# Row tiles of a mixture-of-experts loop loaded by transposing DMAs, with VectorE joining the 16-bit pieces and 15 tiles combined on TensorE

## What is computed

```python
logits = h @ gate_w.T                    # 2048 tokens, 32 experts
scores = sigmoid(logits)                 # groups of experts limit the choice
tki    = top 8 experts of each token     # tkw: their weights, scaled by 2.5
g = silu(einsum('th,eih->tei', h, w_gate))
u = einsum('th,eih->tei', h, w_up)
routed = einsum('tei,ehi->th', g * u * combine[:, :, None], w_down)
shared = (silu(h @ sh_gate.T) * (h @ sh_up.T)) @ sh_down.T
out    = x + routed + shared
```

## Time and profile before

| | |
|---|---|
| time, median of 3 runs | 613.6 us (612.79 to 614.25) |
| the profiled execution, its own time | 612.29 us |
| its span, first to last instruction | 611.0 us |
| mean granted TensorE clock | 0.976 |
| busy share PE / DVE / ACT / POOL | 92% / 67% / 61% / 59% |

### The profile page before, as it was taken

One profiled execution on the slowest core, in us unless ns is written; L12 is line 12 of the kernel. 1 busy time (PEld: TensorE's weight loads), 2 busy tenths in 40 slices (PEclk: granted clock), 3 DMA queues, 4 the chain that ended last, 5 costly groups with the idle time before them and its releaser, 6 DMA issues.

```text
span 611.0 us, 11524 instructions
## 1 busy us (share of the span) xinstructions
PE 563.9 (92%) x2677; PEld 422.3 (69%) x2677; DVE 407.4 (67%) x1554; ACT 372.3 (61%) x993; POOL 361.8 (59%) x414
## 2 busy tenths in 40 slices
PE   3989989889999798798997999999999999999996
PEld 2666557655766455555666888888788888888875
DVE  6975675986768987647776444444444444688897
ACT  1867888868786755552611666566566666677760
POOL 4343233632143377876777777777777777777730
PEclk9979999999999899899799999999999999999999
DMA  8999300000000023239364999876666666999966
GB/s 258 394 397 383 131 0 2 1 1 0 2 0 0 17 92 119 98 119 343 119 222 167 304 321 342 293 223 214 200 202 205 209 207 198 346 412 407 411 255 222
DMA packets 62063, 119.69 MB, mean 196 GB/s; under 512 B 8667, under 2 KB 45583, under 8 KB 59951
## 3 DMA queue, kind: packets, MB, share of 16 engines
q1 hardware_dynamic: 48079, 77.63, 37.5%
q0 software_dynamic: 13488, 41.04, 17.7%
q10 hardware_dynamic: 432, 0.29, 0.3%
HBM read 61.29 MB, written 57.64 MB: 195 GB/s over the span
## 4 chain that ended last, share of the span: by engine, by line
PE 78%; DVE 10%; ACT 6%; DMA 3%; issue 1%; POOL 1%; SPq 0%; DVEq 0%; POOLq 0%; ACTq 0%
PE ps L2023 22%; PE ps L2043 11%; PE ps L1671 7%; PE ps L1656 6%; PE ps L1882 5%; PE ps L1682 5%; PE ps L1695 5%; PE ps L2036 3%; PE ps L1642 3%; PE ps L1777 3%; PE ps L1783 2%; DVE tokrow L750 2%; PE ps L1794 2%; DMA arena<-yrows 2%; DMA xs<-in_x 1%
## 5 line engine op out<-in xcount | busy, mean ns | idle before, releaser
L2023 PE MATMUL ps<-arena,mats 128*128 x636 | 164.0, 381 | 0.3 <-issue 0.3
L609 POOL DMA_INDIRECT xrows<-tokrow,place_of x128 | 125.2, 978 | 41.8 <-issue 37.5
L1267 DVE TENSOR_TENSOR mats<-ps,mats 128x128 f32<-128x128 f32 x159 | 46.3, 291 | 106.1 <-ACT mats L1453 101.1
L2023 PEld LDWEIGHTS ps<-arena,mats 128*128 128x128 f32 x636 | 108.6, 191 | 8.8 <-issue 0.5
L2043 PE MATMUL ps<-arena,mats 128*128 x318 | 95.5, 383 | 1.0 <-DVE mats L1274 1.0
L1453 ACT ACTIVATE mats<-ps 128x128 f32<-128x128 f32 x159 | 44.1, 277 | 56.4 <-PE ps L2023 56.4
L1446 ACT COPY mats<-ps 128x256 f32<-128x256 f32 x159 | 58.0, 365 | 11.9 <-PE ps L1882 11.9
L1387 ACT ACTIVATE hat<-tokrow,total 128x256 f32<-128x256 f32 x96 | 47.6, 499 | 18.8 <-DVE tokrow L815 11.7
L1395 ACT ACTIVATE hat<-tokrow,shift,rstd 128x256 f32<-128x256 f32 x96 | 49.7, 591 | 12.9 <-POOL shift L540 12.8
L2043 PEld LDWEIGHTS ps<-arena,mats 128*128 128x128 f32 x318 | 48.0, 191 | 13.7 <-issue 2.1
L545 POOL TENSOR_SCALAR var_eps<-variance 128x4 f32<-128x4 f32 x24 | 6.4, 269 | 83.5 <-ACT hat L1387 83.2
(11 more groups left out here) (237 smaller groups left out, 1136.0 us busy)
## 6 DMA issues: line engine op xcount, KB each, us to landing
hat<-xrows SPq DMA_DIRECT2D x81, 160.0 KB
rows<-xrows SPq DMA_DIRECT2D x78, 160.0 KB
arena<-in_experts SPq DMA_DIRECT2D x4, 1920.0 KB, 18.8
xrows<-padrow SPq DMA_DIRECT2D x32, 160.0 KB
hat<-yrows SPq DMA_DIRECT2D x5, 1024.0 KB, 8.4
tokrow<-yrows SPq DMA_DIRECT2D x5, 1024.0 KB
hatT<-yrows SPq DMA_DIRECT2D x5, 1024.0 KB, 8.9
xrows<-padrow SPq DMA_DIRECT2D x1, 4960.0 KB
```

Of the source, the lines that this page charges most:

```text
L609: gp.indirect_dma_start(out=xrows[:, :], out_offset=bass.IndirectOffsetOnAxis(ap=place_of[:, g, k:k + 1], axis=0), in_=tokrow[:, g, :], in ...
L2023: mm = te.matmul(bank(6 + u)[:, 0:2 * I], turned_row[u][:, dc * P:(dc + 1) * P], arena[:, dc * D:(E - 1) * WCOL + (dc + 1) * D][:, bass.ds ...
```

## The change

1. **Row loads.** The 256 token values of a tile are loaded by `dma_start_transpose`, which works on 16-bit elements: a row is 512 halves, and the tile arrives as `[128 partitions, 4 chunks, 128 rows]` of halves, already turned. The 64 other columns come by a second, plain DMA. Each row load is thus two DMAs on the same queue, and a row buffer is ready at a count of 32 in place of 16.
2. **Halves.** For this, each token row is stored with all the low halves first and then all the high halves. ScalarE writes the normalised tokens into `hat` and a new operation `halve(i)`, once per block, rearranges 4 x 512 halves per partition into `tokrow`. `dispatch` and the first `shared_silu` of the block wait for it. TensorE turns the tokens from `hat`.
3. **TensorE** has no `turn_row` and no PSUM bank for it. `copy_row` is now the joining of the two halves of each value, SBUF to SBUF, 512 elements of 16 bits per partition with a step of two on the output; VectorE does it up to tile 134, ScalarE from tile 135 (`SHIFT_AT`). `copy_act` is ScalarE's for every tile.
4. **15 tiles kept.** `KEPT` goes from 6 to 15, so tiles 144 to 158 are not scattered. Their products (`combine`) stand inside TensorE's loop, two stages after `down`, with six sets of 0/1 matrices in turn.
5. **Tables.** `ASK_AT` and `SUM_AT` are set anew, ten token tiles are asked for after SyncE's last row load, and the last reload has no buffer of its own: it waits, as the others do, for the sum three tiles before it.

```diff
-KEPT = 6
-SHIFT_AT = 116
+KEPT = 15
+TOKEN_SETS = 6
+SHIFT_AT = 135
-ASK_AT = [128, 129, 133, 136, 139, 142, 145, 148, 152, 155, 158]
-SUM_AT = [120, 123, 126, 129, 132, 135, 138, 141, 145, 148, 151, 154]
+ASK_AT = [140, 141, 149, 156, 157, 158]
+SUM_AT = [133, 136, 142, 148, 149, 150, 152, 153, 155, 156, 157, 158]
...
                 if g == EARLY_SUMS:
                     wait_scattered(TILES - KEPT)
-                if g == EARLY_SUMS + 3:
-
-                    sy.wait_ge(down_done, TILES)
-                    sy.dma_start(last_back, results[g]).then_inc(row_in[0], 16)
-                    return
...
                 if n >= ROWBUFS:
-                    sy.wait_ge(row_turned, n - ROWBUFS + 1)
+                    sy.wait_ge(row_copied, n - ROWBUFS + 1)
                     sy.wait_ge(own_ready, (n - ROWBUFS) // GROUP + 1)
-                sy.dma_start(rowbuf[n % ROWBUFS], xrows[bass.ds(at[n % 4], P), :]).then_inc(row_in[n % ROWBUFS], 16)
+                sy.dma_start_transpose(rowhalf[n % ROWBUFS], halves[bass.ds(at[n % 4], P), 0:2 * D]
+                                       ).then_inc(row_in[n % ROWBUFS], 16)
+                sy.dma_start(rowbuf[n % ROWBUFS][:, WTS:ROW], xrows[bass.ds(at[n % 4], P), WTS:ROW]
+                             ).then_inc(row_in[n % ROWBUFS], 16)
...
+            def halve(i):
+                ac.wait_ge(normed[i // Q], past(i, 2 * ROUNDS, TQ))
+                ac.copy(slots[:, set_of(i), :].bitcast(HALF).rearrange("p t (h d) -> p t h d", h=2),
+                        hat[:, set_of(i), :].bitcast(HALF).rearrange("p t (d h) -> p t h d", h=2)).then_inc(halved, 1)
...
+            def copy_row(s):
+                u = s % 2
+                ve.wait_ge(row_in[s % ROWBUFS], 32 * (s // ROWBUFS + 1))
+                if s >= 2:
+                    ve.wait_ge(gate_up_done, s - 1)
+                ve.tensor_copy(turned_row[u].bitcast(HALF).rearrange("p (n h) -> p h n", h=2),
+                               rowhalf[s % ROWBUFS].rearrange("p (h c) r -> p h (c r)", h=2)).then_inc(row_copied, 1)
...
+            def combine(k):
+                n = TILES - KEPT + k
+                te.wait_ge(token_known, k + 1)
+                te.wait_ge(y_ready, n + 1)
+                for t in range(TQ):
+                    mm = te.matmul(bank(4 + t // 2)[:, t % 2 * D:(t % 2 + 1) * D], of_token[k % TOKEN_SETS][:, t, :],
+                                   ybuf[y_place(n)], start=k == 0 and t % 2 == 0, stop=k == KEPT - 1 and t % 2 == 1)
+                mm.then_inc(combined, 1)
...
-            for n in range(TILES + 3):
-                if 1 <= n < TILES:
-                    turn_row(n)
+            for n in range(TILES + 5):
...
+                if TILES - KEPT + 5 <= n:
+                    combine(n - 5 - (TILES - KEPT))
```

More of the change, by code:

```diff
@@ L7 @@
 I32 = mybir.dt.int32
+HALF = mybir.dt.uint16
 ALU = mybir.AluOpType
@@ L255, in build @@
             "p (k d) -> p k d", k=TOPK), hatT[0].rearrange("p c (k d) -> p (c k) d", d=D)]
-        last_back = place(arena, 0, TOPK, D)
         of_token = [part(hatT[1][:, :, :], k * TQ * P, TQ, P) for k in range(4)]
-        of_token += [part(tokrow[:, :, :], k * TQ * P, TQ, P) for k in range(KEPT - 4)]
+        of_token += [part(tokrow[:, :, :], k * TQ * P, TQ, P) for k in range(TOKEN_SETS - 4)]
         into_token = part(mats[:, 4, :, :], GROUP * E * 3, GROUP)
@@ L502, in sync_program @@
                 ask_back(g)
+                if g == T and T >= len(ASK_AT):
+                    store(0, TQ)
                 if g == EARLY_SUMS - 1:
@@ L605, in dispatch @@
                     gp.wait_ge(weighed, 2 * (i + 1))
-                    gp.wait_ge(normed[i // Q], past(i, 2 * ROUNDS, TQ))
+                    gp.wait_ge(halved, i + 1)
                 g = i * TQ + step // 4
@@ L1322, in add_kept @@
                 if half == 0:
-                    ve.wait_ge(combined, 1)
+                    ve.wait_ge(combined, KEPT)
+                    ve.wait_ge(out_ready, EARLY_SUMS + TQ)
                 g = EARLY_SUMS + 2 * half
-                at = (4 + 2 * half) * BANK
-                ve.tensor_tensor(xs[:, g:g + 2, :], ps[:, at:at + 2 * BANK].rearrange("p (b c) -> p b c", b=2)[:, :, 0:D],
-                                 xs[:, g:g + 2, :], ALU.add).then_inc(out_ready, 2)
+                ve.tensor_tensor(xs[:, g:g + 2, :], bank(4 + half).rearrange("p (t d) -> p t d", t=2),
+                                 xs[:, g:g + 2, :], ALU.add).then_inc(out_ready, 1)
             starts = [tiles_from(phase) for phase in range(3)]
             for n in range(TILES + 2):
+                if n < SHIFT_AT:
+                    copy_row(n)
                 if 1 <= n <= TILES:
@@ L1392, in normalise @@
                 ac.wait_ge(shift_ready[i // Q], past(i, n))
-                into = hat if n < 2 * ROUNDS else slots
                 for g in tiles_of(i):
-                    ac.activation(into[:, g, :], source[:, g, :], ACT.Identity, bias=shift[:, g:g + 1],
+                    ac.activation(hat[:, g, :], source[:, g, :], ACT.Identity, bias=shift[:, g:g + 1],
                                   scale=rstd[:, g:g + 1]).then_inc(normed[i // Q], 1)
@@ L1467, in copy_out @@
                     u = y_last(n) // YGROUP
-                    ac.wait_ge(scattered[u % YGROUPS], 16 * YGROUP * (u // YGROUPS + 1))
+                    ac.wait_ge(scattered[u % YGROUPS],
+                               16 * sum(m // YGROUP % YGROUPS == u % YGROUPS for m in range(min(YGROUP * (u + 1), TILES - KEPT))))
                 ac.wait_ge(own_ready, n // GROUP + 1)
@@ L1579, in scalar_program @@
             score_tokens(0)
+            halve(0)
             evacuate(3, 3)
@@ L1589, in scalar_program @@
             score_tokens(1)
+            halve(1)
             normalise(3, 4, slots)
@@ L1607, in scalar_program @@
             score_tokens(2)
+            halve(2)
             normalise(3, 2 * ROUNDS, xs)
@@ L1611, in scalar_program @@
             score_tokens(3)
+            halve(3)
             shared_silu(2, 1)
```

97 lines of the change are left out of this document (35 added, 62 removed).

## The result

| | before | changed |
|---|---|---|
| median (range, runs) | 613.92 us (612.79 to 616.09, 4) | 748.04 us (745.68 to 753.58, 4) |
| ratio | | 1.219 (95%: 1.211 to 1.227) |
| span, mean granted clock | 611.0 us, 0.976 | 748.1 us, 0.919 |

The forecast was 606.3 us with a range to 628. The change makes the kernel 22% slower; the prediction had given such a side a chance of 0.28 and no price over 653.

A forecast was written before the change was run, and what follows sets the result against it. TensorE and GpSimd were both taken as full and ending together; on GpSimd's path 611.0 - 11.4 + 1.1 + 3 = 603.7, plus 1.3 us twice, made 606.3 us, range 600.5 to 628.

The forecast's parts named there:

- I take it as hidden: SyncE's row loads: a pair hides up to 1.43 us a tile, so the transposing load was given no cost.
- The first rival: SyncE's queue or DMA engines: transposing loads set the pace from 1.48 us a pair, up to 652 us; chance 0.21.
- Up to about 1.0 fits beside the scatters: DMA engines: a tile's load takes 0.54 us of their time, and about 1.0 us would fit.
- TensorE would end at 586.1.: TensorE's kept products: end at 605.3, less 35.0 us of transposes, plus 15.8 us for nine more kept tiles.
- With the same 24.05 us behind it.: After the loop: last scatter starts at 575.6, the unchanged 24.05 us follow, and the span ends at 599.6.
- The GpSimd path: GpSimd's scatters to the end: nine fewer save 11.4 us, which limits the gain; 603.7 with the added costs.
- I take 3 us, near that row: GpSimd's DMAs beside VectorE's new row copy: total lengthening taken as 3 us, near the L804 row's no cost.
- as the adds: Row copy holding GpSimd's DMAs like VectorE's two-input adds: 0.05 to 0.15 us each, 7 to 23 us.
- The row of L804: VectorE's L804 beside a dispatch at 241.84, which keeps its 0.96 us: read as the copy costing GpSimd nothing.
- The second rival: VectorE's copy shuts GpSimd out for its whole length: +0.33 us for each of 150 DMAs, 653 us; chance 0.06.
- TensorE's tile of 1.40 and VectorE's chain: In the loop: TensorE's tile falls from 1.62 to 1.40 us; VectorE's chain of 1.3 to 1.9 mostly fits 1.77.
- the third rival: The loop doesn't reach 1.40: VectorE's chain leaves 1.44 to 1.47 us a tile, 614 us; chance 0.09.

The follow-up runs named there:

- plain_pair: The change with its transposing load replaced by a plain load of the same 256 columns, rows unturned: 640.08 us, ratio 1.045 to the kernel before.
- two_chunks: The change with the transposing load bringing two of four chunks and the copy reading a constant: 747.04 us, ratio 1.217 to the kernel before.
- values_on_scalar: The change in full, with the plain loads issued by ScalarE's queue and the transposing ones by SyncE's: 659.79 us, ratio 1.073 to the kernel before.
- early8_third: plain_early8 repeated beside a kernel before of 613.25 us: 632.90 us, ratio 1.031.
- copies_kept6_again: plain_pair with row copies on ScalarE, the sums' places of before and six kept tiles: 618.18 us against 615.36, ratio 1.0049.
- four_plain: plain_pair with the 256 columns brought by three plain loads, so four issues a tile: 767.6 us, ratio 1.251 to the kernel before.
- plain_early8: plain_pair with the sums and their loads placed earlier, nearly as before: 764.75 us beside a kernel before of 722.24 us, ratio 1.060.

## Why the prediction was wrong, point by point

- **"The transposing load may cost some 1.5 to 1.8 times a plain one before it counts. ... I take it as hidden."** This is the step that failed. The bound was right, 1.43 us a pair; the value inside it was a choice, without a row. The issue is 1.20 us, three times the 0.41 of the plain one next to it. In the prediction's own measure, from one start to the next, it is 1.41 us where 0.58 was a plain one's, and the pair with its register work is 2.0 to 2.4 where 1.43 would have been hidden. `plain_pair` shows that this is 108 us, `two_chunks` that half the bytes don't make the issue cheaper, `values_on_scalar` that 88 come back once the two loads have separate queues.
- **The first rival** had the mechanism, the place and the point of decision (1.48 us a pair), and its signature (a queue without gaps), but "at twice the plain issue" bounded the price at 1.74 a pair and 652 us. With the measured 2.18 of a tile without a pad its own formula gives 312 + 149 x 2.18 + 21.6 = 658 for tile 149 (its load is issued at 665.8), and with the 59 us that the forecast has behind it 717. So the price and the chance of 0.21 were wrong, and some 30 of the 748 us are again not in the formula: the chain that ended last has only reloads and VectorE's work from 684.80, where the row loads are nearly through, to the end, since ten token tiles are asked for after the last row load.
- **The bytes of the loads.** "Up to about 1.0 fits beside the scatters" was not the limit in the change (share 0.54). In `values_on_scalar` the share is 0.96, beside a queue that still hardly waits.
- **"TensorE would end at 586.1."** With free loads it ended at 628.7, 41.5 us late even after the 1.1 of `halve`. From the table: it starts 7.5 us later, not 1.1 (the first dispatch alone, which was taken as covered, starts at 213.4 in place of 210.58; where the rest comes from was not looked into); between tiles 0 and 130 it needs 194.6 us where 212.8 - 28.6 = 184.2 were counted, and between tiles 0 and 50 nearly nothing is gained (80.5 us against 81.8), while `pick` waits 8.9 us for plain loads among the pads; and behind tile 130 it needs 91.8 where 57.7 - 6.4 + 15.8 = 67.1 were counted. The nine kept tiles were sized about right, as `early8_third` has them (3.13 - 1.40 = 1.73 each against 1.755). What was missing is that TensorE can't use its lead: the two paths were summed as if independent, but y buffers and reloads tie it to GpSimd's scatters.
- **"With the same 24.05 us behind it."** True where six tiles are kept: 25.0 and 24.9. With fifteen it is 53 us in `plain_pair`, where the late reloads and sums come last, and 45 in `early8_third`, where TensorE's kept products do. The GpSimd path was counted with a tail that belonged to other places of the sums and another number of kept tiles.
- **"I take 3 us, near that row"** for VectorE's copy against GpSimd: measured 587.0 - 577.5 = 9.5 us at the last scatter, inside the 7 to 23 of "as the adds" and not near L804's nothing. The reckoning for the adds was the right one: hit by the share of time that a copy runs, 0.455/1.40, and held for half its length gives 0.07 us each, and the 89 DMAs from 410 to 530 are 0.08 longer on average. The row of L804 was misread. That operation starts at 242.06, 0.22 us after its dispatch, and so could not show a hold, while the add at 538.72 was running when its scatter started: it ends at 540.01, the scatter 0.82 behind it.
- **The second rival** charged each of 150 DMAs with a whole copy, 0.33 us; that price is refuted by the 0.08. The mechanism is not: a DMA that starts into a copy is held until the copy ends. The Trainium skill (SBUF — State Buffer, "SBUF: two separate sides") says that of a VectorE operation in a two-port mode and a GpSimd operation the one that starts first has the shared port pair for the whole instruction. The trace agrees, with the 49 held DMAs and the 67 of 76 that start before a copy and take less than 1.00; whether this copy runs in such a mode no run shows.
- **TensorE's tile of 1.40 and VectorE's chain**: right (501.55 and 502.95; 1.41 over long stretches of `plain_pair`), so the third rival is out. `copy_row` took 0.455 us in the bounds of 0.37 to 0.65.
- **Which path ends it.** That at most the GpSimd path's share of the 35 us would come through was right in kind, and too hopeful in size: `copies_kept6_again` is what remains, none.

## What to carry to other kernels

A DMA of a kind that the trace doesn't show has a price on the queue that issues it, apart from its bytes; if the loop's slack is known (here 1.43 us a tile), measure the issue first or let the range reach what three or four times a plain one would give. When two engines end together, freeing one gives little (here nothing), and their paths may not be added up apart: look for the buffers and reloads by which the faster one is held to the slower. A row in which two operations overlap shows a contention only if they overlap in the order that matters: look which of them started first. Work moved behind the last wait (here kept products) comes at full price at the end.

## What the runs showed of the hardware

- A transposing DMA mostly occupies SyncE's queue for 1.17 to 1.23 us (medians 1.18 to 1.21), whether it brings two chunks or four; a plain one 0.33 to 0.42. From start to start it costs nearly as much as the three plain ones of `four_plain` (1.41 against 1.55 us).
- An indirect DMA on GpSimd that starts while VectorE's 16-bit copy from SBUF to SBUF runs ends 0.80 us behind the copy (49 of 51 in `plain_pair`), up to 1.21 us in place of 0.96; one that starts before its copy is mostly not lengthened (67 of 76 under 1.00, 481.22 above). The same shows beside the two-input adds of the kernel before, 0.82 us behind at 539.45. With a copy of 0.455 us every 1.40 us this is 0.08 us per DMA on average.
- The kernel before took 613 to 615 us in four comparisons (the record names chips 0 and 6) and 720 to 722 in three others (chips 12, 3 and 4). The profiles beside the latter show long idle times for no wait, on VectorE 75.6 us before `product` from 300 to 600 in `plain_early8`; in `plain_early8` SyncE's issues, 0.52 us apart in `plain_pair`, are up to 2.9 apart:

```profile
410.32 0.71 SPq L487 DMA_DIRECT2D rows<-xrows  x1
411.06 0.36 SPq L498 DMA_DIRECT2D xrows<-padrow  x1
413.25 0.71 SPq L485 DMA_DIRECT2D rows<-xrows  x1
416.11 0.71 SPq L487 DMA_DIRECT2D rows<-xrows  x1
```

The cause is open, and each kernel is judged only against the kernel before of its own comparison.
